# Writing the zeros of empty expert places at the third to fifth value tile instead of the last three

## The reference, cut to what matters

```
xn = layernorm(x)                               # x: 2 x 1024 x 512, float32
# attention, one head of width 512
q, k, v = split(xn @ w_qkv.T + b_qkv)
s = softmax(q @ k.T / sqrt(512)) @ v @ w_out.T + b_out
# mixture of experts, 8 experts, the best 2 for each of the 2048 tokens
logits = xn @ router_w + router_b
w = softmax(top2(logits))
combined = sum over the chosen e of w_e * silu(xn @ expert_w[e] + expert_b[e])
y = xn + combined @ proj_w + proj_b
g = silu(norm_w * y / rms(y))
out = x + s * g
```

## Time and profile before

| | |
|---|---|
| median of 3 runs | 489.4 us (488.75 to 489.73) |
| the profiled execution's own time | 489.93 us |
| its span in the profile | 488.2 us |
| PE busy | 474.4 us, 97% |
| DVE / ACT / POOL busy | 316.4 / 213.6 / 218.0 us |
| DMA | 115.77 MB, mean 237 GB/s |

### The profile page before, as it was taken

One profiled execution on the slowest core, in us unless ns is written; L12 is line 12 of the kernel. 1 busy time (PEld: TensorE's weight loads), 2 busy tenths in 40 slices (PEclk: granted clock), 3 DMA queues, 4 the chain that ended last, 5 costly groups with the idle time before them and its releaser, 6 DMA issues.

```text
span 488.2 us, 7198 instructions
## 1 busy us (share of the span) xinstructions
PE 474.4 (97%) x2152; PEld 388.6 (80%) x2153; DVE 316.4 (65%) x472; ACT 213.6 (44%) x310; POOL 218.0 (45%) x317
## 2 busy tenths in 40 slices
PE   6899999999999999989999999999999999999995
PEld 3788786888888878878888888888888878888884
DVE  3966252677653426969888888752597754857762
ACT  2674553142331153736444444332655441644550
POOL 4586110006887849603000000745567873377134
PEclk9999999999999999999999999999999999999999
DMA  8865999947979599896996666897454864445512
GB/s 303 304 235 197 381 374 378 390 155 257 301 262 345 183 319 308 252 259 209 261 286 204 188 196 196 298 310 276 155 158 165 275 183 154 146 145 174 173 41 90
DMA packets 78142, 115.77 MB, mean 237 GB/s; under 512 B 6608, under 2 KB 36320, under 8 KB 78112
## 3 DMA queue, kind: packets, MB, share of 16 engines
q1 hardware_dynamic: 65072, 79.72, 51.6%
q0 software_dynamic: 6896, 23.36, 13.6%
q10 hardware_dynamic: 6144, 12.32, 7.2%
HBM read 66.09 MB, written 49.28 MB: 236 GB/s over the span
## 4 chain that ended last, share of the span: by engine, by line
PE 72%; POOL 9%; DVE 7%; issue 4%; DMA 4%; ACT 1%; SPq 1%; DVEq 0%; ACTq 0%; POOLq 0%
PE ab L1646 19%; PE ab L1647 18%; PE ab L1648 18%; POOL rows_scratch L794 6%; PE sc L1646 4%; PE sc L1647 4%; PE sc L1648 4%; POOL W L783 3%; PE tp L1652 2%; DMA rows_scratch<-xb,pos 2%; DMA raw_v<-in_w_qkv 2%; PE tp L1688 1%; PE sc L1717 1%; DVE stats L1206 1%; DMA xs<-p_scratch 1%
## 5 line engine op out<-in xcount | busy, mean ns | idle before, releaser
L811 POOL DMA_INDIRECT y<-y_scratch,pos x32 | 33.2, 1036 | 87.8 <-DMA y_scratch<-yt_so 74.1
L1646 PE MATMUL ab<-W,st_h 128*128 x156 | 60.8, 390 | 1.5 <-DVE st_l L1343 1.5
L1648 PE MATMUL ab<-W,st_l 128*128 x156 | 60.7, 389 | 0.0
L1647 PE MATMUL ab<-W,st_h 128*128 x156 | 60.7, 389 | 0.0
L794 POOL DMA_INDIRECT rows_scratch<-xb,pos x32 | 31.3, 977 | 51.0 <-DVEq L1331 42.8
L1646 PE MATMUL sc<-xt_h,t_h 128*128 128x512 f32 x128 | 50.1, 391 | 0.0
L1648 PE MATMUL sc<-xt_h,t_l 128*128 128x512 f32 x128 | 49.8, 389 | 0.0
L1647 PE MATMUL sc<-xt_l,t_h 128*128 128x512 f32 x128 | 49.8, 389 | 0.0
L1070 ACT CAST st_h<-tp 128x512 fp32r<-128x512 f32 x39 | 22.9, 587 | 41.0 <-PE ab L1648 38.9
L1646 PEld LDWEIGHTS ab<-W,st_h 128*128 128x128 f32 x156 | 29.3, 188 | 8.0 <-issue 1.9
L1410 DVE TENSOR_REDUCE small<-sc 128x1 f32<-128x1024 f32 x16 | 19.5, 1222 | 24.1 <-PE sc L1648 23.9
(11 more groups left out here) (284 smaller groups left out, 1225.0 us busy)
## 6 DMA issues: line engine op xcount, KB each, us to landing
rows_scratch<-xn ACTq DMA_DIRECT2D x3, 3328.0 KB, 20.1
xb<-in_expert_w POOLq DMA_DIRECT2D x6, 1024.0 KB
xn<-rows_scratch SPq DMA_DIRECT2D x48, 128.0 KB, 3.4
xg<-rows_scratch SPq DMA_DIRECT2D x44, 128.0 KB
y_scratch<-yt_own SPq DMA_DIRECT2D x20, 256.0 KB, 2.8
y_scratch<-yt_so SPq DMA_DIRECT2D x19, 256.0 KB, 2.7
p_scratch<-prob SPq DMA_DIRECT2D x9, 512.0 KB
rows_scratch<-xs SPq DMA_DIRECT2D x16, 256.0 KB, 6.6
```

What stands on the lines that cost most here:

```text
L811: pool.indirect_dma_start(y[:, q, :], None, y_d, bass.IndirectOffsetOnAxis(pos[:, GB * s + p:GB * s + p + 1], 0))\
L1646: nc.tensor.matmul(dst, lh, rh, start=start, stop=False)
L1647: nc.tensor.matmul(dst, lh, rl, start=False, stop=False)
L1648: return nc.tensor.matmul(dst, ll, rh, start=False, stop=stop)
```

## The change

The three calls of `clear_slots` keep their size, their queue and their order. They move in ACT's program from behind `v_hi(0, 5)`, `v_hi(0, 6)`, `v_hi(0, 7)` to behind `v_hi(0, 2)`, `v_hi(0, 3)`, `v_hi(0, 4)`.

```diff
@@ -957,9 +957,9 @@
                 if 1 <= t < 5:
                     qk_high(t - 1)
                 v_hi(0, t)
-                if t >= GB - 3:
+                if 2 <= t < 5:
                     act.wait_ge(zero_set, 1)
-                    clear_slots(t - GB + 3)
+                    clear_slots(t - 2)
             act.wait_ge(ln_done, 3)
             for g in range(GB, GB + 4):
                 normalise(g)
```

## The result

The changed kernel takes 495.84 us (median of 5 runs, 494.78 to 498.47) against 489.4 us before; the ratio of the two is 1.0143, 95% interval 1.0117 to 1.0169, so it is slower by some 7.0 us by the ratio, 6.4 by the medians. The profiled execution took 497.03 us, its span is 495.3 us.

The account below looks back on a forecast made before the run. PE, busy 474.4 of 488.2 us, was taken to bound the kernel. Late values +5.2, removed hold 0 and moved traffic 0 on 489.93 gave 495.1, or 494.6 us on the median's footing; range 492.3 to 497.2.

Parts of the forecast that it names:

- Which view bounds the kernel: Whole kernel: PE's busy time and waits bound it; what PE loses near 43 us arrives at the end.
- The third issue is held: Third zero issue on ACT, expected at 39.65 us: held again, taking 5 to 7 us.
- about one transfer's worth has drained: Reason for the hold's end: tied to the first zero transfer's draining, 11.23 us after the first issue without other traffic.
- Rival B: Third issue at 39.65 us takes 0.4 us, no hold, kernel stays at 489.4 us; chance 0.08.
- When it ends: End of ACT's hold on the third zero issue: 46.2 us, between 44.2 and 46.9.
- 2.0 us for the traffic beside it: Addition to the hold for 1.03 MB of x load and row stores, out of 2.7 us if all goes ahead.
- taking turns and the order of arrival: Two rules for SP's stores beside the zeros; taking turns adds nearly their whole 2.7 us, order of arrival less.
- What stands behind it: ACT's `normalise(7)`, `hi(6)`, `v_hi(0, 5)` start late, so `values(0, 6)` starts at 48.3, 5.2 us late.
- Rival A: PE's clock falls in the new gap near 47 us, 2.2 us more: 496.8 us; chance 0.20.
- the 4.3 us wait at the start: PE's first wait, for weights, said to leave the clock full; used as evidence against a fall in the new gap.
- one term, +5.2: PE's late start of `values(0, 6)`, 5.2 us, the only nonzero part of the sum.
- What moving the traffic gives: Earlier zeros and less crowded DMA from 65 to 95 us: 0 to 0.5 us gained, taken as 0.

Follow-up runs that it names:

- e1: Changed kernel with the third zero write back at tile 7, the first two still at tiles 2 and 3: 489.65 us, ratio 1.0009 to the kernel before.
- e5: Changed kernel with zero writes of 10, 4 and 25 row tiles instead of 13 each, same places: 488.79 us, ratio 1.0000 to the kernel before.
- e4: Changed kernel with zero writes of 1, 19 and 19 row tiles instead of 13 each: 492.01 us, ratio 1.0056 to the kernel before.
- e2: Changed kernel with the third zero write at tile 5, the first two at tiles 2 and 3: 493.05 us, ratio 1.0068 to the kernel before.
- e6: Kernel before, zeros at their old place, with 23 unread matmuls added on PE ahead of `turn(7)`: 496.81 us, ratio 1.0167.
- e9: Kernel before with 12 short unread float32 matmuls (48 instructions) in front of everything on PE: 493.89 us, ratio 1.0094.
- e12: All three zero writes, 13 tiles each, issued by SP instead of ACT, behind the store of row tile 4: 498.95 us, ratio 1.0196 to the kernel before.
- e8: Changed kernel with 18 unread matmuls filling PE's wait ahead of `turn(7)`: 496.72 us, ratio 1.0162 to the kernel before.

## Why the prediction was right, and where it was not

**Which view bounds the kernel, and that PE's place in the value loop reaches the end:** right. 8.3 us at the first send (121.23 against 112.95), 6.9 at the last matmul. It is not the same shift all the way, as the forecast had it.

**The third issue is held:** right, at 40.37 for 6.77 us, and e1 and e5 show that the loss hangs on this alone. My reason, "about one transfer's worth has drained", gave the right time by luck, as all three were of one size; e4 broke it, and e5 confirmed what took its place. Rival B (no hold) is out; its argument that a wider spacing might do was sound in kind, as e5 shows, but 0.6 us are some 110 pieces.

**When it ends:** 2.0 us for the traffic beside it came out nearly right, and in part by luck. First issue to end of hold took 13.57 us; the forecast had 13.2, and 11.23 before, so 2.34 us were added. But SP's queue moved 1.51 MB in that stretch and not 1.03, and all queues together moved 405 GB/s over it, against 348 over the 11.23 us before and the 381 of the forecast. So the 2.34 us do not decide between taking turns and the order of arrival.

**What stands behind it:** forecast 5.2 us, measured 4.71 + 0.81 = 5.52 in one trace and 5.62 in the other. `values(0, 7)` did follow without a wait, and `normalise(8)` was in time.

**Rival A was not a rival but what happened.** This is the step of the prediction that failed. I gave the clock's fall 0.20, on the ground that the 4.3 us wait at the start left the clock full. That was misread: the first matmuls ran at 1.2 GHz until 9.06 us, by their own spacing of 0.85 us against 0.43, and the page's 9 in the first slice and the view's 1.00 stand for a time without a record. Read so, the start speaks for rival A and not against it. Both traces of the changed kernel have the low stretch, and the mean granted clock of its ten timed runs is 0.989 to 0.995, against 0.994 to 1.0 in 52 runs of the kernel before. The forecast for case A was 496.8; by the ratio the kernel takes 496.4, by its median 495.84. e2 makes it plainer: the clock fell after a wait of 2.4 us.

The Trainium skill's page "TensorE: Matmul & The Clock Gate", section "Part 1: The HAM clock gate (the "warmup" mystery)", says that an idle PE loses the full clock and gets it back only by work. By that rule the traces agree, in the middle of the kernel and at its start: the clock was back at 54.6 us after PE had been at work since 48.1, and at 9.06 after work since 4.33.

**The time inside the range is in part luck.** The sum had one term, +5.2, and nothing for the clock or for what is given back. In the trace the hold's path was +5.52 and the clock +2.25, and -1.07, -0.82 and +0.3 followed near 180, 218 and 328 us; the missing terms have opposite signs.

**What moving the traffic gives:** forecast 0, and e5 has 1.0000. The prediction found no wait of PE between 36 and 168 us that earlier zeros could save. Behind that stretch there is one, of 0.9 us near 180 in the trace before, and it is gone in all seven traces with at least the first zero writes early and no added instructions, with steps of -1.03 to -1.07 us, in e1 and e5 too, where PE was not late. e6 and e9, with the zeros at their old place, lack 0.7 and 0.4 us of it. The timed runs of e1 and e5 gain nothing over before, so either it is not in every execution of the kernel before or it is given back later (e1 loses 1.8 us near 320 us, e5 does not); the runs do not show which.

## What to carry to other kernels

A large DMA is not free for the engine that issues it: look at the duration of the issuing instruction, and at what the queue still holds in front of it. Moved to a place where the engine has work that PE needs, a hold of 5 us that cost nothing became one of 6.8 us that cost 5.5 and the clock on top; sizing the transfers so that less is left ahead of the next one removed it without moving anything. A granted clock of 1.00 at the start of a trace may be a time without a record: compare the durations of equal matmuls before resting a rival on it. A filler that is meant to measure an effect needs a control with as many instructions elsewhere, as its own side effect here was as large as what it was to measure.

## What the runs showed of the hardware that was not expected

- An issue on ACT's queue was held until 1272 to 1437 pieces of 2 KB were left ahead of it, whatever its own size (nine long holds and five short ones; one more ended with 1219 left); it took 0.4 us with 1481 or fewer left at its start and 0.96 us with 1537. In SP's queue a hold of 8.56 us on a store of only 128 pieces ended with 1415 left, but stores issued back to back behind it with 1276 and 1408 left still took 1.2 us (e12).
- The granted clock fell in waits of PE of 4.6 and 4.7 us (both traces of the changed kernel), after one of 2.4 us (e2), in e2 only once PE was at work again, and not with the wait of 1.3 us in e4. In e8 it fell a microsecond after a wait of 1.9 us, and in e6 with no wait over 0.6 us near it.
- Behind its first wait of 4.3 us PE ran at 1.2 GHz until 9.06 us (matmuls 0.85 us apart, then 0.43), where the view prints 1.00 because there is no record.
- One 16 KB packet of the instruction queue beside a store of 512 KB made its landing 5.1 us instead of 2.8, the store's last 16 pieces coming singly behind the packet; 48 extra PE instructions at the start cost 4.6 us in all (ratio 1.0094, 1.0067 to 1.012), of which the packet is up to 2.2.
